# Two conditioned transformer layers in one kernel: set-up reordered and its weight handling moved into the steps

## The chip, the cores and the metric

The kernel runs on one core of a Trainium2 chip. The metric is the device time of one execution in microseconds. The core's engines are TensorE (PE: matrix products and transposes), VectorE (DVE), ScalarE (ACT), GpSimd (POOL) and SyncE (SP), which here only issues transfers (DMA). Each engine works through its own instructions in order and they meet through semaphores.

## What is computed

128 sequences of 64 tokens, 256 features, go through two layers. Both are attention with 16 heads of 16 features and a feed-forward part of width 1024, with a layer norm before each that is scaled and shifted by a condition vector (one of 256 features per sequence). All inputs are float32.

```python
# layer 0
gamma1 = cond @ g1_w + g1_b;  beta1 = cond @ b1_w + b1_b          # "modulation", also gamma2, beta2
alpha1 = tanh(cond @ a1_w + a1_b) * 0.1                           # "gate", also alpha2
y = layernorm(x, ln1_g, ln1_b) * (1 + gamma1) + beta1
x = x + attention(y, qkv_w, qkv_b, proj_w, proj_b) * alpha1
z = layernorm(x, ln2_g, ln2_b) * (1 + gamma2) + beta2
x = x + (gelu(z @ fc1_w + fc1_b) @ fc2_w + fc2_b) * alpha2
# layer 1
h = layernorm(x, ln1_g, ln1_b) * (1 + scale) + shift              # [shift, scale] = cond @ ada1_w + ada1_b
q, k = rotary(h @ wq + bq), rotary(h @ wk + bk);  v = h @ wv + bv
x = x + softmax(where(mask, q k^T / 4, -inf)) v @ wo + bo
x = x + gelu(ada_norm2(x) @ ff_w1 + ff_b1) @ ff_w2 + ff_b2
```

## The kernel before

**Precision.** Weights and activations are split in a high and a low part (`wgt_hi`, `wgt_lo`, `y_hi`, `y_lo` ...), and a product is three passes (helper `product`, L886). The high part of a weight is made by a copy on ScalarE (`high_weights`, L656 and L659), the low part by a subtraction on VectorE (`low_weights`, L1187 and L1191). `w_hi[n]` and `w_lo[n]` count what is done, with n = 0 for qkv, 1 for the projection, 2 for fc1 and 3 for fc2. A feed-forward matrix has 2048 columns per partition, the projection 512, qkv 1536. There is one copy of the split weights: layer 1's overwrite layer 0's.

**Tiling.** The 8192 tokens make 16 tiles of 512 (8 sequences) per layer, so 32 tiles in all, and `NT` = 16. Layer 0's result goes to memory (`mid`) and is read again by layer 1. A **step** u works on up to five tiles at once: it loads and normalises tile u+2 (argument `n`), makes y, queries, keys and values of tile u+1 (`a`), runs attention of tile u (`b`), feed-forward of tile u-1 (`c`) and finishes tile u-2 (`p`). Each argument is the layer of that tile, or None where there is no such tile. The order of all of it is written out by hand in one `step` function per engine. The whole kernel is, on every engine, `begin`, step -1, `second`, step 0, `third`, step 1, a loop over steps 2 to 13, steps 14 to 17, a loop over steps 18 to 29, and steps 30 to 33 (function `program`). Step -1 makes y, queries, keys and values of tile 0; step 0 is attention of tile 0 without any feed-forward; layer 1's tiles begin to appear as tile u+1 in step 15.

**Attention.** A tile has four groups of two sequences. Queries and keys of a group are spread into padded buffers by transfers: four for the keys (`spread_keys`, L418) and two for the queries (`spread_queries`, L426), with two sets of buffers, so groups 0 and 1 are sent at the end of the step before and groups 2 and 3 early in the step itself. The scores of a group (PE, `A<-k_pad,q_pad`) wait for them. Then come maximum (L1335) and subtraction (L1341) on VectorE, the exponential (L749) on ScalarE, transposes (L1022), a copy (L754), weighing of the values (L1036), normalising (L1359), a transpose of the heads (`turn_heads`, L1047), the projection, and the gated residual on VectorE.

**Set-up.** `begin` loads the condition, tile 0, weights, biases; makes the transposed condition, layer 0's first modulation (TensorE L897 into bank D0, VectorE `modulations`, L1199 to L1206) and the split of qkv. In `second` TensorE makes the gate products (L918, L919), the second modulation and a transpose of the mask (L924); ScalarE copies the projection, takes the tanh (L671) and copies fc1 and fc2 whole; VectorE subtracts the projection, makes the gates, the modulation and the mask, and subtracts fc1 and fc2 whole; SyncE writes the four gate rows and the mask to memory and waits for them (`rows_out`). The rows are broadcast back in every step of layer 0 (L444, L445, L476). In `third` layer 1's modulation weights and columns are loaded (L321 is the line of the small helper `ld` that most loads go through), its modulation is made, its qkv weights are sent for, and all engines wait for all of it before step 1.

**The turn to layer 1.** Layer 1's qkv is split in step 15 (`u == NT - 1`) before the first product of the feed-forward, the projection early in step 16. fc1 is split whole between two softmaxes of step 17, fc2 some 20 us later in that step.

## Time and profile before

| what | value |
|---|---|
| median of 3 runs | 1927.71 us (1926.1 to 1930.4) |
| profiled execution | 1930.19 us |
| its span | 1928.4 us, 41731 instructions |
| mean granted TensorE clock | 0.98 |
| PE busy | 1806.2 us (94%) |
| DVE, ACT, POOL busy | 1235.5 (64%), 1307.8 (68%), 849.7 us (44%) |
| chain that ended last | PE 66%, DVE 13%, issue 10%, POOL 7%, ACT 2% |
| queries to their buffer (`q_pad<-q_flat`) | 256 transfers of 128 KB, 2.3 us to landing |

Times in all views are in us from the start of the span. A row of a timeline gives the start, the duration, the engine, the line, the operation, what it writes and reads, how often (neighbours are merged), and in brackets how long the engine had been idle and who released it. Matrix products are pipelined, so a row's duration is a little longer than its share of the engine. The granted clock is a share of 2.4 GHz: 1.00 is that level all the time, 0.50 would be 1.2 GHz all the time.

### The profile page before, as it was taken

The page shows a single profiled execution, that of the slowest core. Times are in us where ns is not written, and L with a number is a line of the kernel's source. Part 1 is how long each engine was busy: PE and PEld are TensorE (multiplying, and loading weights), DVE is VectorE, ACT ScalarE, POOL GpSimd, SP SyncE. Part 2 cuts the span into 40 slices and gives each one's busy share as a digit, 9 for nine tenths or more (in the row PEclk, how much of TensorE's full clock was granted, in tenths as well). Part 3 has the DMA queues.
Part 4 walks back from the last instruction along what each step waited for, and adds up shares of the span by engine and source line. Part 5 has one row for each costly group of instructions (what it writes and reads, how often), then busy time and mean ns, then how long its engine had stood idle before and what let it go on. Part 6 is the DMA issues. An engine that isn't in the chain of part 4 may idle for free.

```text
span 1928.4 us, 41731 instructions
## 1 busy us (share of the span) xinstructions
PE 1806.2 (94%) x12623; PEld 1646.5 (85%) x12623; DVE 1235.5 (64%) x2973; ACT 1307.8 (68%) x2315; POOL 849.7 (44%) x1036
## 2 busy tenths in 40 slices
PE   5779999999999999999897999999999999999997
PEld 4668988888898888889787989999988998998985
DVE  5656666767666676766676567767666766766651
ACT  3347776776777677777666676776676677677663
POOL 2123333343333334334544565555555555556433
PEclk8879999999999999999998999999999999999999
DMA  6464434444443444543343233333323333332320
GB/s 162 110 138 103 102 97 114 120 121 129 104 100 98 111 120 122 128 107 96 109 142 95 73 93 103 97 102 106 92 81 104 97 96 105 110 82 85 98 60 33
DMA packets 330275, 199.84 MB, mean 104 GB/s; under 512 B 160994, under 2 KB 314596, under 8 KB 330212
## 3 DMA queue, kind: packets, MB, share of 16 engines
q1 hardware_dynamic: 330212, 199.06, 38.8%
q8 instruction: 32, 0.52, 0.1%
q14 instruction: 31, 0.25, 0.0%
HBM read 80.98 MB, written 17.33 MB: 51 GB/s over the span
## 4 chain that ended last, share of the span: by engine, by line
PE 66%; DVE 13%; issue 10%; POOL 7%; ACT 2%; DMA 1%; SPq 1%; DVEq 0%; POOLq 0%; ACTq 0%
PE D L886 16%; PE C L886 12%; PE A L886 12%; PE B L1036 7%; PE B L886 7%; PE B L1022 4%; PE E L886 3%; POOL h_lo L551 2%; DVE mx L1335 2%; POOL q_flat L597 2%; DVE o_sb L1359 2%; PE A L1008 2%; DVE exps L1341 1%; DVE ot_lo L1368 1%; PE E L1047 1%
## 5 line engine op out<-in xcount | busy, mean ns | idle before, releaser
L551 POOL TENSOR_TENSOR h_lo<-hact,h_hi 128x512 fp32r<-128x512 f32 x256 | 330.5, 1291 | 325.0 <-ACT h_hi L745 317.0
L886 PE MATMUL D<-wgt_hi,h_hi 128*128 128x256 f32 x1024 | 304.2, 297 | 27.3 <-POOL h_lo L551 18.6
L886 PE MATMUL D<-wgt_lo,h_hi 128*128 128x256 f32 x1024 | 290.7, 284 | 0.0
L886 PE MATMUL D<-wgt_hi,h_lo 128*128 128x256 f32 x1024 | 290.4, 284 | 0.0
L886 PE MATMUL A<-k_pad,q_pad 128*128 128x256 f32 x1536 | 260.9, 297 | 9.8 <-DVE mod L1206 4.7
L740 ACT ACTIVATE hact<-C,b_col 128x512 f32<-128x512 f32 x256 | 176.2, 688 | 124.0 <-PE C L886 121.8
L1036 PE MATMUL B<-v_blocks,probs_turned 128*128 128x68 f32 x2048 | 255.8, 272 | 0.0
L1036 PEld LDWEIGHTS B<-v_blocks,probs_turned 128*128 128x128 f32 x2048 | 250.7, 193 | 5.2 <-ACT probs_turned L754 2.5
L754 ACT COPY probs_turned<-B 128x512 f32<-128x512 f32 x256 | 147.8, 585 | 157.1 <-PE B L1022 157.0
L886 PEld LDWEIGHTS D<-wgt_hi,h_hi 128*128 128x128 f32 x1024 | 196.1, 191 | 44.5 <-POOL h_lo L551 29.8
L886 PEld LDWEIGHTS A<-k_pad,q_pad 128*128 128x128 f32 x1536 | 215.6, 195 | 13.8 <-DVE mod L1206 4.9
L1335 DVE TENSOR_REDUCE mx<-A 128x8 f32<-128x512 f32 x256 | 174.3, 681 | 79.2 <-PE A L1008 48.6
L886 PE MATMUL C<-z_hi,wgt_hi 128*128 128x512 f32 x512 | 210.6, 411 | 6.1 <-ACT hact L740 4.7
L749 ACT ACTIVATE exps<-exps 128x512 f32<-128x512 f32 x256 | 161.2, 630 | 79.7 <-DVE exps L1341 79.0
L886 PE MATMUL C<-z_hi,wgt_lo 128*128 128x512 f32 x512 | 201.1, 393 | 0.0
L886 PE MATMUL C<-z_lo,wgt_hi 128*128 128x512 f32 x512 | 200.5, 392 | 0.0
L886 PEld LDWEIGHTS D<-wgt_hi,h_lo 128*128 128x128 f32 x1024 | 196.7, 192 | 1.3
L886 PEld LDWEIGHTS D<-wgt_lo,h_hi 128*128 128x128 f32 x1024 | 196.3, 192 | 0.0
L1341 DVE TENSOR_TENSOR exps<-A,mx 128x512 f32<-128x512 f32 x256 | 173.9, 679 | 3.8 <-PE B L1022 0.5
L541 POOL TENSOR_SCALAR rs<-mv 128x1 f32<-128x1 f32 x128 | 30.0, 234 | 323.8 <-DVE mv L1392 321.2
L1022 PE MATMUL B<-ident,exps 128*128 128x128 f32 x1024 | 157.3, 277 | 8.4 <-DVE o_sb L1359 5.2
L1359 DVE TENSOR_TENSOR o_sb<-B,rden 64x128 f32<-64x128 f32 x512 | 146.5, 286 | 24.9 <-PE E L1047 7.7
(138 smaller groups left out, 4231.5 us busy)
## 6 DMA issues: line engine op xcount, KB each, us to landing
k_pad<-k_flat SPq DMA_DIRECT2D x512, 64.0 KB, 2.1
q_pad<-q_flat SPq DMA_DIRECT2D x256, 128.0 KB, 2.3
gates<-gates SPq DMA_DIRECT2D x64, 256.0 KB, 4.5
x_bias<-x_bias SPq DMA_DIRECT2D x32, 512.0 KB, 3.5
rotation<-rotation SPq DMA_DIRECT2D x256, 64.0 KB, 1.9
x_in<-in_x SPq DMA_DIRECT2D x16, 512.0 KB, 4.2
gates<-gated_bias SPq DMA_DIRECT2D x32, 256.0 KB, 4.9
x_res<-in_x SPq DMA_DIRECT2D x16, 512.0 KB, 4.2
```

Source lines behind the costliest of these rows:

```text
L551: pool.tensor_tensor(hb[1][:, m % 2, :], hact[:, m % 2, :], hb[0][:, m % 2, :].bitcast(F32), ALU.subtract).then_inc(h_lo, 1)
L597: pool.tensor_tensor(flat[keys][:, :, i % KC, 1, :], by_group(rot_sum[:, i % KC, :]), flat[keys][:, :, i % KC, 0, :].bitcast(F32), ALU.sub ...
L740: nc.scalar.activation(hact[:, m % 2, :], C[:, :], ACT.Gelu, bias=b1_col[:, layer, m:m + 1]).then_inc(gelu, 1)
L749: nc.scalar.activation(exps[:, b, :], exps[:, b, :], ACT.Exp, scale=SCORE_SCALE).then_inc(s_exp, 1)
L754: nc.scalar.copy(pt[:, b, :], B[b][:, :]).then_inc(pt_moved, 1)
L886: ins = nc.tensor.matmul(dst, l, r, start=first_start and n == 0, stop=last_stop and n == len(todo) - 1, **kw)
L1008: ins = nc.tensor.matmul(dst, mean_w[:, :], row, start=False, stop=True)
L1022: ins = nc.tensor.transpose(B[b][:, n * P:(n + 1) * P], exps[:, b, n * P:(n + 1) * P], ident[:, :])
L1036: ins = nc.tensor.matmul(B[b][:, n * 68:(n + 1) * 68], pt[:, b, n * P:(n + 1) * P], moving, start=True, stop=True)
L1335: nc.vector.tensor_reduce(mx[:, b, :], A[b][:, :].rearrange("p (h k) -> p h k", k=S), AX.X, ALU.max)\
L1341: nc.vector.tensor_tensor(exps[:, b, :].rearrange("p (h k) -> p h k", k=S), A[b][:, :].rearrange("p (h k) -> p h k", k=S), mx[:, b, :].rea ...
L1359: ins = nc.vector.tensor_tensor(o_sb[p, b, :].rearrange("p (n j d) -> p n j d", n=4, j=2), sums_of(b)[p, :, x, :, 0:HD], rden[p, b, :].rea ...
```

## The change

- **Loads of `begin`.** The mask is loaded early, qkv next, then the gate and second modulation weights ahead of the bias columns. Bias columns of the modulations get semaphores of their own (`cols_in`), which VectorE waits for and TensorE doesn't. fc1 and fc2 leave `begin` and are issued at the start of `second`, ahead of the gate rows.
- **GpSimd** clears the key buffers before the first layer-norm chain and not after it.
- **Step -1** takes over what `second` did: TensorE makes mask transpose, gate products and second modulation right after y's transposes and before the queries (`gate_products`); ScalarE casts qkv before it waits for the modulation; VectorE subtracts the query and key weights after y's shift, the value weights apart (`low_values`, semaphore `w_lo_v`), and makes mask and gates there (`gate_parts`). Group 0's queries are sent before group 1's keys. The mask goes to memory alone (`mask_out`).
- **Step 0** takes over what `third` did, and the feed-forward weights: layer 1's modulation weights and columns are loaded after group 3 (`modulation_weights`, 10 transfers, into other buffers), TensorE makes both modulations right after y's transposes, VectorE scales both modulations, and fc2 and fc1 are split in pieces of a quarter (512 columns, `high_piece`, `low_piece`) spread over the step. The load of `x1_bias` for tile 0 moves to its end.
- **Step 1** ends, on SyncE, with layer 1's 16 query and key columns (`layer_columns`); **step 14** ends with the other columns, rows and the qkv and projection weights (`layer_weights`), and ScalarE and VectorE split qkv at its end and not in the middle of step 15.
- **Steps 16 and 17** split layer 1's fc1 and fc2 in quarters: five at the end of step 16, three in step 17, each as soon as the last tile of layer 0 has used that quarter. TensorE waits per quarter.

```diff
@@ SyncE
             def begin():
                 ...
-                columns(mods_in[0], 0, 0, [w[0]["g1_b"], w[0]["b1_b"]])
+                columns(cols_in[0], 0, 0, [w[0]["g1_b"], w[0]["b1_b"]])
+                ld(mask_in, mask_u8[:, :], t["mask_BxS_bf1"])
                 ld(w_in[0], qkv, rows(w[0]["qkv_w"]))
-                qk_columns(0, [w[0]["qkv_b"][0:2 * D]])
-                other_columns(0, w[0]["qkv_b"][2 * D:3 * D], w[0]["fc1_b"])
-                projection(0, w[0]["proj_w"])
                 for n, m in enumerate(("a1", "a2")):
                     ld(gates_in, mod_raw[4 + n], rows(w[0][m + "_w"]))
                     ld(gates_in, gate_row[:, n, :], row(w[0][m + "_b"]))
+                for n, m in enumerate(("g2", "b2")):
+                    ld(mods_in[1], mod_raw[2 + n], rows(w[0][m + "_w"]))
+                qk_columns(0, [w[0]["qkv_b"][0:2 * D]])
+                projection(0, w[0]["proj_w"])
                 ld(gates_in, bias_rows[:, 0, :], w[0]["proj_b"].partition_broadcast(P))
                 ld(gates_in, bias_rows[:, 1, :], w[0]["fc2_b"].partition_broadcast(P))
                 ...
+                other_columns(0, w[0]["qkv_b"][2 * D:3 * D], w[0]["fc1_b"])
+                columns(cols_in[1], 0, 1, [w[0]["g2_b"], w[0]["b2_b"]])
+
+            def second():
+                ld(w_in[3], w_raw[2].rearrange("p (k n) -> p k n", k=MC), rows(w[0]["fc2_w"]))
                 ld(w_in[2], w_raw[1].rearrange("p (k n) -> p k n", k=KC), rows(w[0]["fc1_w"]))
                 ...
                 sp.wait_ge(gates_made, 4)
                 ...
-                sp.wait_ge(mask_made, 3)
-                ld(rows_out, mask_rows, mask_add)
-                sp.wait_ge(rows_out, 80)
-                sp.wait_ge(mod_done, 16)
+                sp.wait_ge(rows_out, 64)
+                sp.wait_ge(pe_mods, 2)
+
+            def modulation_weights():
+
+                sp.wait_ge(pe_gates, 1)
                 for n in range(2):
                     ld(mods_in[2], ada_raw[n], rows(w[1][f"ada{n + 1}_w"]))
                     ...
@@ SyncE, step
                     spread_keys(u, 3)
                     spread_queries(u, 3)
+                if known(u) and u == 0:
+                    modulation_weights()
                 ...
                     spread_keys(u + 1, 0)
-                    spread_keys(u + 1, 1)
+                    if not (known(u) and u == -1):
+                        spread_keys(u + 1, 1)
                     wait_apart(sp, sp_passed, (qk_hi, upto(u + 1, 4, 4)), low_done(u + 1, a, 4))
                     spread_queries(u + 1, 0)
+                    if known(u) and u == -1:
+                        spread_keys(u + 1, 1)
                     spread_queries(u + 1, 1)
+                if known(u) and u == 0:
+                    wait_apart(sp, sp_passed, (w_lo[3], 4))
+                    gated_bias(0)
+                if known(u) and u == 1:
+                    layer_columns()
+                if known(u) and u == NT - 2:
+                    layer_weights()
@@ ScalarE, step
-                if known(u) and u == NT - 1:
-                    act.wait_ge(pe_v, upto(NT, 2, 0))
-                    high_weights(0, 1)
                 ...
                 if c is not None:
                     hidden(u - 1, c, 2)
+                elif known(u) and u == 0:
+                    high_piece(3, 0, 0)
                 ...
+                if known(u) and u == NT - 2:
+                    act.wait_ge(pe_v, upto(NT, 2, 0))
+                    high_weights(0, 1)
+                if known(u) and u == NT:
+                    high_piece(3, 1, 1)
+                    high_piece(2, 1, 2)
                 if n is not None:
                     first_norm(u + 2)
                     first_columns(u + 2, n)
@@ TensorE, step
                 if a is not None:
                     first_turn(u + 1, 0, b)
                     first_turn(u + 1, 1, b)
+                if known(u) and u == -1:
+                    gate_products()
+                if known(u) and u == 0:
+                    pe.wait_ge(mods_in[2], 16 * 2)
+                    pe.wait_ge(mod_done, 16)
+                    for n in range(2):
+                        modulations(Dk[n], ada_raw[n][:, :, D:2 * D], ada_raw[n][:, :, 0:D])
                 if b is not None:
                     turn_heads(u, 1, c)
@@ VectorE
             def low_weights(n, layer):
                 dve.wait_ge(w_hi[n], layer + 1)
                 if n == 0:
-                    for kind in W_PIECES:
+
+                    for kind in W_PIECES[1 - layer:]:
                 ...
+            def low_piece(n, layer, q):
+                dve.wait_ge(w_hi[n], 4 * layer + q + 1)
+                nc.vector.tensor_tensor(ff_piece(n, wgt[1][:, W_AT[n]], q), ff_piece(n, w_source(n, layer), q),
+                                        ff_piece(n, wgt[0][:, W_AT[n]], q).bitcast(F32), ALU.subtract).then_inc(w_lo[n], 1)
@@ VectorE, step
+                if known(u) and u == NT:
+                    low_piece(2, 1, 0)
+                    low_piece(2, 1, 1)
+                    low_piece(3, 1, 0)
+                    low_piece(3, 1, 1)
+                    low_piece(2, 1, 2)
```

## Rows read from the trace of the kernel before

**Rows 1.** Stages: length; each engine's busy us; clock; DMA share; GB/s.

```profile
core 0: us, PE busy (x) PEld busy (x) DVE busy (x) ACT busy (x) POOL busy (x), PEclk, DMA share, GB/s
...
46.45:97.10 50.65, 37.92 (x232) 33.71 (x232) 34.64 (x80) 19.26 (x39) 7.28 (x14) 0.83 0.46 107
97.10:113.70 16.60, 6.75 (x33) 6.48 (x32) 5.83 (x20) 3.05 (x8) 3.36 (x4) 0.74 0.24 45
113.70:174.03 60.33, 57.63 (x367) 52.38 (x368) 35.36 (x88) 38.86 (x70) 15.88 (x23) 0.90 0.50 118
174.03:230.19 56.16, 54.44 (x386) 49.44 (x385) 37.53 (x92) 40.79 (x73) 20.80 (x27) 1.00 0.45 114
904.49:968.36 63.87, 57.49 (x389) 52.67 (x388) 43.06 (x101) 42.84 (x79) 32.12 (x40) 0.95 0.44 116
...
1028.08:1098.90 70.82, 59.88 (x403) 55.32 (x402) 43.34 (x94) 44.23 (x74) 33.55 (x39) 0.90 0.28 79
1098.90:1155.67 56.77, 55.68 (x403) 51.35 (x401) 37.77 (x90) 40.52 (x73) 31.70 (x39) 1.00 0.34 98
```

**Rows 2.** Timeline of TensorE in the set-up.

```profile
24.06 0.77 PE L886 MATMUL A<-y_hi,wgt_hi 128*128 128x512 f32 x1 [10.58 <-DVE y_lo L1282]
...
35.62 1.03 PE L918 MATMUL C<-gates,condT 128*128 128x256 f32 x4
...
38.89 2.05 PE L897 MATMUL D<-condT,gates 128*128 128x128 f32 x16
...
46.45 2.93 PE L886 MATMUL A<-k_pad,q_pad 128*128 128x256 f32 x12 [0.38 <-DVE maskT L1243]
```

**Rows 3.** Layer 0's modulation scaled on VectorE (line view), and GpSimd's memset (timeline).

```profile
L1206 DVE TENSOR_SCALAR mod<-mod,ln_col x4: 278/278/1905, 13.3 to 44.9; 128x128 f32<-128x128 f32 x4
...
13.19 1.92 POOL L516 MEMSET v_blocks<- 128x2176 f32 x1
```

**Rows 4.** Timeline of SyncE: the eight columns, and the first gate load.

```profile
5.28 5.22 SPq L321 DMA_DIRECT2D qk_bias<-in_L_cond_qkv_b  x8
...
47.02 0.66 SPq L444 DMA_DIRECT2D gates<-gates  x1
```

**Rows 5.** DMA issues up to 125 us: count, KB each, us to landing.

```profile
q_pad<-q_flat SPq DMA_DIRECT2D x14, 128.0 KB, 2.4
...
x_bias<-in_L_cond_fc_w SPq DMA_DIRECT2D x1, 1024.0 KB, 9.3
...
rotation<-in_L_cond_ada_w SPq DMA_DIRECT2D x2, 512.0 KB, 3.7
...
mask_u<-in_mask_BxS_bf SPq DMA_DIRECT2D x1, 8.0 KB, 9.0
```

**Rows 6.** Timeline of TensorE in step 0 and before step 1.

```profile
59.24 0.96 PE L886 MATMUL A<-k_pad,q_pad 128*128 128x256 f32 x6
...
102.36 6.67 PE L897 MATMUL D<-condT,rotation 128*128 128x128 f32 x32 [5.17 <-DMA mod_col<-in_L_cond_ada_b]
113.70 1.65 PE L886 MATMUL A<-k_pad,q_pad 128*128 128x256 f32 x6 [4.67 <-DVE mod L1206]
```

**Rows 7.** Timelines about a step's end: SyncE, ScalarE, VectorE.

```profile
890.78 2.78 SPq L426 DMA_DIRECT2D q_pad<-q_flat  x4
902.12 0.65 SPq L444 DMA_DIRECT2D gates<-gates  x1
...
851.17 0.63 ACT L749 ACTIVATE exps<-exps 128x512 f32<-128x512 f32 x1
...
917.98 1.86 ACT L656 CAST wgt_hi<-w_raw 128x512 fp32r<-128x512 f32 x5
...
1155.87 0.69 DVE L1335 TENSOR_REDUCE mx<-A 128x8 f32<-128x512 f32 x1 [3.16 <-PE A L1008]
```

**Rows 8.** Timelines of step 17: ScalarE and VectorE.

```profile
1034.33 1.90 ACT L659 CAST wgt_hi<-w_raw 128x2048 fp32r<-128x2048 f32 x1
...
1036.27 2.29 DVE L1191 TENSOR_TENSOR wgt_lo<-w_raw,wgt_hi 128x2048 fp32r<-128x2048 f32 x1 [2.95 <-ACT wgt_hi L659]
...
1058.62 2.26 DVE L1191 TENSOR_TENSOR wgt_lo<-gates,wgt_hi 128x2048 fp32r<-128x2048 f32 x1
```

212 lines of the change are left out of this document (133 added, 79 removed).

## Prediction

> **What bounds the kernel now.** I read the stages first [rows 1]. From 174 us on a tile of layer 0 takes 56.16 us, in 54.44 of which TensorE is busy at full clock, and one of layer 1 takes 56.77: there TensorE is the bound, and the change adds and removes next to no product. What it can win lies where TensorE waits. That is four places: the set-up up to the first scores at 46.45 us; step 0 (50.65 us long, 37.92 busy, clock 0.83); 16.60 us between its last product and step 1, with 6.75 busy; and steps 15 and 17 at the turn to layer 1 (63.87 and 70.82 us, 7.1 and 14.1 over the steady 56.77). I then read TensorE's own idle rows in the set-up [rows 2], who disturbs VectorE there [rows 3], SyncE's queue [rows 4, 7] and the landings [rows 5], since all transfers go through that one queue.
>
> **Set-up, before the first scores.** TensorE idles 10.58 us until y is made at 24.06 [rows 2]. Three edits shorten y's path. TensorE's modulation product no longer waits for the bias columns (0.7 us, from the 4 column loads issued after the two weights). One VectorE instruction of layer 0's modulation took 1.91 us where its three twins take 0.28, over the very time of a 1.92 us memset on GpSimd [rows 3]; with the key memsets moved to the start, that overlap goes: 1.6 us. The subtraction of the query and key weights (1.4 us) comes after y's scale and shift, not before, so it moves but stays on the path; only the values' part leaves it. Together y is ready near 19.8. But the gate products now stand ahead of the queries in TensorE's order, and their semaphore counts six transfers, the two broadcast bias rows among them. In SyncE's new order these come behind the 8 query/key columns, which alone cost 5.22 us of issue [rows 4]; adding up the queue, they are issued by 15.6 and land near 18.9. The products took 3.3 us at full clock (35.62 to 38.89); at 1.2 GHz, where TensorE starts after such a wait, 1.6 times that (32 products in 6.67 us against 16 in 2.05) [rows 2, 6]: 5.4, and the second modulation 2.05. So queries begin at about 26.5, 2.4 us later than now; they then run at full clock and end with the values near 35.5, where they end now. Up to here nothing is won. What is won is the stretch from 35.62 to 46.45 [rows 2]: products, mask and the two whole-matrix subtractions are gone from it, and the group's queries are sent ahead of the second group's keys. First scores: about 37.5, 9 us earlier.
>
> **The same 9 us, lost again.** fc2 and fc1 (1 MB each) are now issued near 39.7, directly ahead of the four gate rows; SyncE waits for those rows before it issues anything of step 0. In the trace an 8 KB mask issued behind the same two weights took 9.0 us to land, as long as the weight ahead of it (9.3) [rows 5]. So the rows land near 50.3; now SyncE goes on at 47.02 [rows 4]. Then come, at 0.66 us of issue each, four gate loads, the third group's four keys and two queries, 6.6 us, and the last lands 2.4 later [rows 5]: 59.4 with the small gaps between. The third group's scores run at 59.24 now [rows 6]. TensorE gets there 9 us early and stands still. Gain at this point: 0 (below: 0 if rows drain faster is wrong; above: 7, if the small rows overtake the weights). I take 0 by the mask row. The Trainium skill (DMA: Bandwidth & Descriptors, Queues, rings and completion order) says that each DMA engine consumes its ring's descriptors in order while completion is not first-in first-out for the issuing engine; by the first half the 9 us are lost, by the second some could stay, and the mask row speaks for the first.
>
> **Step 0, second half.** TensorE now stops after y's transposes until layer 1's two modulation weights are in. SyncE issues them behind the fourth group (near 62.0), the second one five issues later, landing 3.7 us on [rows 5]: 68.9, where TensorE arrives at 67 to 68. The products take 3.4 us at full clock, 6.67 at 1.2 GHz [rows 6]. Everything queued behind them waits: the second group's heads, and through them VectorE, whose shifts for y stand behind those heads. Shift against now: 5 to 8 us, I take 5.1. On VectorE come layer 1's 16 modulation instructions (4.67 us, as long as TensorE waits for them now) [rows 6] and layer 0's eight, half that: the eight fall into the wait for the third group and cost nothing; the 16 are half hidden while TensorE makes the first keys, and eight pieces of 512 columns at about 0.65 us (a quarter of the 2.29 us whole [rows 8], plus start-up), half hidden in its idle time; on ScalarE eight pieces of about 0.55, mostly hidden. That is 3.5 more: step 0 ends 8.6 us later than now, near 105.7.
>
> **Between step 0 and 1.** The 16.60 us go entirely: 5.17 waiting for a column, 6.67 of products, 4.67 waiting for VectorE [rows 6]. Step 1 starts at 105.7 instead of 113.7, gain 8.0. It loses 0.8 again, since normalising tile 2 and two pieces now stand right ahead of its first softmax, and wins 4: step 1 runs at clock 0.90 now [rows 1], 10% of 60 us in slow columns, and would start at full clock. **Gain of set-up, step 0 and step 1 together: 11** (3 to 22; the lower end if TensorE runs the modulation slowly and each piece shows in full, the upper if the rows overtake).
>
> **Columns in step 1.** Sixteen issues are twice the 5.22 us row, 10.4 us, where SyncE idles from 893.56 to 902.12 in a steady step, 8.6 us [rows 4, 7]. The overhang of 1.9 delays gate loads and the third group's keys; the latter wait for scores anyway. Cost 0.3 (0 to 2).
>
> **Steps 14 and 15.** Layer 1's query, key and value cast leaves the middle of step 15, where VectorE is full; I put half of the 7.1 us excess on it, 3.9 (3 to 4.5). It now stands at the end of step 14 on ScalarE, ahead of the normalisation, the gelu and the first exponential, and ScalarE has no gap there: the exponential at 851.17 follows its table load at once [rows 7]. Cast 1.86 us [rows 7], plus some 0.8 waiting: SyncE issues six columns and rows and then the three weights after 893.6, to land near 903. Cost 2.7. Net gain 1.2 (-1 to 4).
>
> **Steps 16 and 17.** Step 16 keeps its own excess (the projection's weights are cast in it as before). In step 17 the whole-matrix cast (1.90) and subtraction (2.29) of fc1 sit between two softmaxes, and fc2's subtraction (2.26) holds the first product back [rows 8]. In pieces, five are done at the end of step 16, where VectorE idles 3.16 us before the next tile's maximum [rows 7]: five at 0.65 are 3.3, cost 0.1, and 0.6 for ScalarE's two. Of the three left, two casts (1.1) fall before an exponential that is not waited for yet, and the subtractions follow y, where VectorE idles for the keys. Left of the 14.1: 1.1. Gain 13 (10 to 14).
>
> **Sum.** 11 - 0.3 + 1.2 + 13 = 25 us. The profiled execution takes 1930.19 (span 1928.4 and 1.8 around it), so 1905; the median of the three runs is 2.5 below it: 1903.
>
> **Rivals.** (1) *The rows overtake, or the two weights drain in half the time*: third group at 52.4 instead of 59.4, the modulation weights 7 earlier, all before it hidden: gain 32, 1896. For: the weights arrive from memory while rows leave for it; against: the mask row. (2) *The turn to layer 1 is not bound by the casts*: the piecewise work at the ends of steps 14 and 16 pushes ScalarE's gelus into the next softmax, and clock drops follow as after 24.06; gain there 4, and 11 - 0.3: 15, 1913. For: ScalarE without a gap [rows 7]; against: VectorE's 3.16 us, and that the two long stalls sit right at the whole-matrix rows. (3) *Slower than before*: TensorE stopped in order for the modulation weights. Price: each us that they land after 68.9 is one us on step 0, with 14 won at the turn and 11 here it decides from 25 us on, i.e. landing after 94. For: ten issues behind three queues' worth of spreads; against: 3.7 us landing. (4) *Pieces do not replace the stall but share it*, gain 3 to 10, 1922. A rule of the Trainium skill (SBUF — State Buffer, SBUF: two separate sides) says that VectorE and GpSimd take a shared port pair by an exclusive lock and the loser blocks. The 1.91 us row agrees. By it the reordered memsets win only what [rows 3] shows, so it changes no rival.
>
> **How the numbers follow.** Forecast (gain 18 to 32) 0.60; rival 1 and beyond 0.14; rival 2 0.14; rival 4 0.05; within 0.2% (3.9 us, about what a measurement of this kernel can tell) 0.04; rival 3 or another cause of a slower kernel 0.03. Range: from the upper end of rival 1 with the turn in full (gain 40, 1888) to a little past rival 2 (gain 11, 1917). Faster 0.93, same 0.04, slower 0.03.
>
> **What would show it.** First scores near 37.5; TensorE idle some 9 us before the third group's scores, which stay near 59; a wait of TensorE on the second modulation weight of 1 to 3 us; step 1 from about 106 at clock near 1; step 15 near 62.5, step 16 as long as before, step 17 near 58 us. Wrong it would be if step 0 lengthens beyond 75 us from the first scores, or if a steady step changes from 56.16 or 56.77 at all, since thirty of them outweigh everything here.

## Result and profile after

| | before | after |
|---|---|---|
| median of the timed runs | 1927.62 us (8 runs, 1924.98 to 1931.4) | 1921.01 us (8 runs, 1919.7 to 1922.54) |
| profiled execution, span | 1930.19, 1928.4 us | 1919.92, 1918.1 us |
| granted clock | 0.980 | 0.986 |

The ratio is 0.9964, 95% interval 0.9955 to 0.9973: the change makes the kernel 6.6 us faster. The forecast was 1903 us with a range from 1888 to 1917. The direction was right, the size was not: 25 us were expected. One execution of one experiment (layer 1's modulation weights in front) was slow, 2479 us at a granted clock of 0.65, and stands in no median.

Stages of the kernel after. The columns are those of [rows 1]; the stretches are the set-up up to the first scores, step 0 up to the third group's scores, the rest of step 0, step 1, a steady step of layer 0, then steps 15, 17, 18, a steady step of layer 1, and step 31.

```profile
core 0: us, PE busy (x) PEld busy (x) DVE busy (x) ACT busy (x) POOL busy (x), PEclk, DMA share, GB/s
0.00:41.12 41.12, 25.05 (x103) 19.87 (x104) 20.53 (x53) 13.37 (x27) 9.29 (x18) 0.83 0.45 115
41.12:62.92 21.80, 6.67 (x52) 6.09 (x52) 8.96 (x22) 6.26 (x12) 0.73 (x3) 0.80 0.82 218
62.92:112.78 49.86, 35.69 (x212) 31.84 (x213) 31.35 (x86) 19.33 (x40) 7.30 (x14) 0.85 0.34 83
112.78:170.63 57.85, 54.25 (x369) 48.59 (x367) 37.77 (x94) 41.84 (x79) 19.80 (x27) 0.97 0.40 101
170.63:226.83 56.20, 54.49 (x387) 49.42 (x385) 37.56 (x92) 40.79 (x73) 20.77 (x27) 1.00 0.46 116
901.17:966.61 65.44, 57.63 (x388) 52.41 (x387) 43.89 (x101) 45.16 (x85) 32.66 (x40) 0.95 0.44 115
1026.35:1084.03 57.68, 55.83 (x402) 51.38 (x401) 40.57 (x96) 42.23 (x76) 33.55 (x41) 1.00 0.36 96
1084.03:1143.18 59.15, 57.05 (x403) 52.84 (x402) 37.79 (x90) 40.40 (x73) 31.01 (x39) 0.97 0.33 95
1199.94:1256.70 56.76, 55.71 (x403) 51.37 (x402) 37.76 (x90) 40.42 (x73) 31.72 (x39) 1.00 0.34 97
1823.62:1875.43 51.81, 48.43 (x339) 43.64 (x338) 27.26 (x68) 31.71 (x52) 18.19 (x21) 0.97 0.19 52
```

The steady steps are what they were (56.20 against 56.16 us, 56.76 against 56.77), so the difference lies in the stages around them. A step is counted from its first transposes of `zn` on TensorE to the next step's, and step 1 from its first scores (113.70 before, 112.78 after):

| stage | forecast gain | gain in the two traces |
|---|---|---|
| up to step 1 | 8.0 | 0.9 |
| step 1 | 3.2 (and -0.3 for the columns) | 2.5 |
| steps 2 to 14 | 0 | 0 |
| steps 14/15 | 1.2 | -1.6 |
| step 17 | 13 | 13.1 |
| step 18 | 0 | -2.4 |
| steps 19 to 30 | 0 | -0.7 |
| step 31 | 0 | -1.6 |
| sum | 25 | 10.2 |

Two things blur this balance. The set-up's length varies from one execution to the next: in the four profiles with the set-up of the kernel after (one of them with 48 empty instructions in it) the first scores of step 1 come between 111.1 and 116.4 us, and in the kernel before and one that shares its set-up at 113.7 and 110.3. So the 0.9 us of the table lie within this spread. And in step 31 the granted clock falls to 0.92 and 0.73 in two 5 us slices without any new wait, which happened in the profiles of some kernels and not in others with the same code there. The profiled execution of the kernel before is 2.6 us above its median, that of the kernel after 1.1 below its own. The medians, 6.6 us apart, say more than the 10.3 of the two profiled executions.

**The set-up of the kernel after.** Timeline of TensorE (start, duration, operation; in brackets the idle time before it and what ended it), then the issues of SyncE, and of the view of the DMA issues up to 125 us the landings of the gate rows.

```profile
20.14 2.05 PE L983 MATMUL C<-gates,condT 128*128 128x256 f32 x4 [7.04 <-DMA exps<-in_L_cond_fc_b]
...
26.42 3.78 PE L959 MATMUL D<-condT,gates 128*128 128x128 f32 x16
29.85 0.62 PE L948 MATMUL A<-y_hi,wgt_hi 128*128 128x512 f32 x1
...
41.12 1.66 PE L948 MATMUL A<-k_pad,q_pad 128*128 128x256 f32 x12 [2.09 <-issue]
...
62.92 1.65 PE L948 MATMUL A<-k_pad,q_pad 128*128 128x256 f32 x6 [10.32 <-DMA q_pad<-q_flat]
```

```profile
43.41 0.64 SPq L329 DMA_DIRECT2D x_bias<-in_L_cond_fc_w  x1
44.10 0.64 SPq L329 DMA_DIRECT2D rotation<-in_L_cond_fc_w  x1
44.79 0.47 SPq L329 DMA_DIRECT2D gates<-hact  x1
...
53.57 0.65 SPq L464 DMA_DIRECT2D gates<-gates  x1
```

```profile
gates<-hact SPq DMA_DIRECT2D x2, 128.0 KB, 7.3
```

TensorE waits 7.04 us for the bias rows before the gate products, runs these and the second modulation at 1.2 GHz (16 products in 3.78 us; the same took 2.05 in [rows 2]), and starts the queries at 29.85. The gate rows then stand behind the 2 MB of fc2 and fc1, take 7.3 us to land, and SyncE does not go on before 53.57 (47.02 in [rows 4]). So the third group's scores come at 62.92, 3.7 us later than before [rows 6].

**The rest of step 0.** TensorE's waits, and the one of VectorE behind the last of them:

```profile
73.23 2.05 PE L959 MATMUL D<-condT,rotation 128*128 128x128 f32 x16 [0.95 <-DMA gates<-in_L_cond_ada_w]
...
82.75 0.77 PE L948 MATMUL A<-y_hi,wgt_hi 128*128 128x512 f32 x1 [3.06 <-DVE y_lo L1350]
...
104.63 0.39 PE L948 MATMUL B<-wgt_hi,y_hi 128*128 128x256 f32 x1 [3.20 <-DVE o_sb L1427]
```

```profile
102.59 0.69 DVE L1267 TENSOR_TENSOR wgt_lo<-rotation,wgt_hi 128x512 fp32r<-128x512 f32 x1 [1.30 <-ACT wgt_hi L688]
```

VectorE works in order: y's low part stands behind the heads and layer 1's modulation (3.06 us of TensorE), and the normalised heads stand behind a piece that ScalarE has not cast yet (3.20 us).

**The boundary of steps 14 and 15.** Timelines of ScalarE, VectorE, GpSimd and TensorE, two slices of 5 us, and the line view of the subtraction (ns, min/median/max of its five instructions):

```profile
901.15 1.87 ACT L694 CAST wgt_hi<-w_raw 128x512 fp32r<-128x512 f32 x5 [2.43 <-DMA w_raw<-in_L_cond_wv]
...
903.06 3.70 DVE L1254 TENSOR_TENSOR wgt_lo<-w_raw,wgt_hi 128x512 fp32r<-128x512 f32 x5 [3.44 <-ACT wgt_hi L694]
...
902.47 2.40 POOL L592 TENSOR_TENSOR x_bias<-x_bias,x_res 128x1024 f32<-128x1024 f32 x1
...
908.70 1.62 PE L948 MATMUL A<-k_pad,q_pad 128*128 128x256 f32 x6 [4.43 <-DVE exps L1409]
...
915.37 0.61 PE L1014 MATMUL E<-ident,zn 128*128 128x128 f32 x4
...
905.45:910.45 5.00, 1.75 (x8) 1.78 (x9) 4.99 (x11) 4.04 (x7) 1.29 (x1) 0.69 0.80 199
910.45:915.45 5.00, 5.00 (x31) 5.00 (x30) 3.83 (x8) 2.78 (x5) 2.37 (x1) 0.62 0.13 30
...
L1254 DVE TENSOR_TENSOR wgt_lo<-w_raw,wgt_hi x5: 411/414/2353, 903.1 to 906.3; 128x256 fp32r<-128x256 f32 x4, 128x512 fp32r<-128x512 f32 x1
```

Four of the five subtractions take 0.41 us, one takes 2.35, over the time of GpSimd's sum of x_bias and x_res. TensorE waits 4.43 us for subtracted scores (the granted clock is 0.69 and 0.62 in the two 5 us slices from 905.45 on, some 3.4 us more), and its second set of transposes of this step (915.37) starts 14.2 us after the step's start; in the kernel before it was 7.3 us. In the traces that have the same code here, the five subtractions take between 2.93 and 5.28 us, as they meet GpSimd's instructions, and step 15 between 64.8 and 67.1 us: its 65.4 is one value of a spread. The stall in the middle of step 15, in the kernel before and in the kernel after:

```profile
927.78 0.55 PE L886 MATMUL E<-wgt_hi,ot_hi 128*128 128x256 f32 x1 [3.38 <-DVE ot_lo L1368]
```

```profile
928.35 0.35 PE L948 MATMUL E<-wgt_hi,ot_hi 128*128 128x256 f32 x1 [0.36 <-DVE ot_lo L1436]
```

### The profile page after: what moved, and what is told of

It is laid out like the page before. It is cut to its first block, busy times and chain, and to the rows that moved or that the text cites. A ratio compares the mean times of both kernels' runs of the same rounds, so it can differ in the third digit from the quotient of the medians.

```text
span 1918.1 us, 41774 instructions
## 1 busy us (share of the span) xinstructions
PE 1801.9 (94%) x12623; PEld 1641.1 (86%) x12623; DVE 1236.7 (64%) x2985; ACT 1307.9 (68%) x2327; POOL 848.8 (44%) x1036
## 4 chain that ended last, share of the span: by engine, by line
PE 65%; DVE 11%; issue 9%; POOL 6%; SPq 4%; DMA 3%; ACT 2%; DVEq 0%; POOLq 0%; ACTq 0%
PE D L948 16%; PE C L948 12%; PE A L948 11%; PE B L1093 7%; PE B L948 7%; PE B L1079 4%; PE E L948 3%; POOL h_lo L581 2%; DVE mx L1403 2%; POOL q_flat L627 2%; DMA rotation<-rotation 2%; DVE o_sb L1427 2%; PE A L1065 2%; DVE exps L1409 1%; SPq L449 1%
## 5 line engine op out<-in xcount | busy, mean ns | idle before, releaser
L948 PEld LDWEIGHTS A<-k_pad,q_pad 128*128 128x128 f32 x1536 | 212.5, 192 | 26.7 <-DMA q_pad<-q_flat 14.2
L776 ACT CAST h_hi<-hact 128x512 fp32r<-128x512 f32 x256 | 159.4, 623 | 4.2
```

The source lines that it names most:

```text
L776: nc.scalar.copy(hb[0][:, m % 2, :], hact[:, m % 2, :]).then_inc(h_hi, 1)
L948: ins = nc.tensor.matmul(dst, l, r, start=first_start and n == 0, stop=last_stop and n == len(todo) - 1, **kw)
```

## Experiments

All are edits of the kernel after unless said otherwise. The ratio is to the kernel before in the same series, with its 95% interval. The interval of a median of four is some 3 us to either side (6.5 for both repairs of SyncE's order together), so two experiments are told apart only where they differ by more; where the text gives a smaller difference, it says so or goes by the traces.

### The turn to layer 1 alone

The kernel before, with layer 1's fc1 and fc2 weights handled in quarters in steps 16 and 17 as in the kernel after, and nothing else of the change:

```diff
                 if known(u) and u == NT + 1:
-                    act.wait_ge(pe_f1, upto(NT, MC, 0))
-                    high_weights(2, 1)
+                    high_piece(2, 1, 3)
+                    high_piece(3, 1, 2)
...
+                if known(u) and u == NT:
+                    high_piece(2, 1, 0)
+                    high_piece(2, 1, 1)
```

> The kernel before, with one part of the change alone: layer 1's fc1 and fc2 are split in quarters at the end of step 16 and in step 17. Theory 1 (the turn to layer 1 wins its 13 us, and set-up and step 15 together give back most of that): step 17 falls from 70.8 to 57.5-58 us, all other steps keep their length, median near 1914.5, faster than the whole change (1921.0). Theory 2 (the traces overstate the turn, since their difference, 10.3 us, is larger than that of the medians, 6.6): median near 1918-1921.

Measured: 1918.06 us (1917.07 to 1919.85), ratio 0.9954 (0.9937 to 0.997). Steps 17 and 18:

```profile
1027.23:1084.83 57.60, 55.84 (x403) 51.39 (x402) 40.55 (x96) 42.34 (x76) 33.51 (x41) 1.00 0.34 97
1084.83:1144.25 59.42, 57.03 (x403) 52.84 (x402) 37.82 (x90) 40.41 (x73) 31.05 (x39) 0.97 0.32 94
```

Step 17 wins 13.2 us as in theory 1, step 18, which theory 1 left alone, loses 2.7, and the median is that of theory 2: 9.3 us are won. The whole change gives 6.6. The intervals of the two ratios overlap, so it is not shown that everything else in the change is a loss (3 us by the medians), but nothing of the 12 us expected from it is seen in the medians.

### fc1's and fc2's weights in front again

```diff
             def begin():
...
                 columns(cols_in[1], 0, 1, [w[0]["g2_b"], w[0]["b2_b"]])
+                ld(w_in[3], w_raw[2].rearrange("p (k n) -> p k n", k=MC), rows(w[0]["fc2_w"]))
+                ld(w_in[2], w_raw[1].rearrange("p (k n) -> p k n", k=KC), rows(w[0]["fc1_w"]))
             def second():
-                ld(w_in[3], w_raw[2].rearrange("p (k n) -> p k n", k=MC), rows(w[0]["fc2_w"]))
-                ld(w_in[2], w_raw[1].rearrange("p (k n) -> p k n", k=KC), rows(w[0]["fc1_w"]))
                 sp.wait_ge(gates_made, 4)
```

> The changed kernel, with the loads of fc2 and fc1 back at the end of the first block of loads, as in the kernel before, so that nothing large stands ahead of the gate rows. Theory 1 (the rows wait behind the two weights in the queue): gate rows land 1.8 us after issue and not 7.3, the third group's scores start near 57 and not 62.9, and step 1 some 5-6 us earlier; median near 1915. Theory 2 (TensorE's in-order stop for the modulation weights takes over): third group near 57, but step 1 only 0-2 us earlier, median 1919-1921.

Measured: 1914.36 us (1912.74 to 1916.64), ratio 0.9938 (0.9922 to 0.9955): 6.6 us less than the kernel after, theory 1.

```profile
55.95 1.65 PE L948 MATMUL A<-k_pad,q_pad 128*128 128x256 f32 x6 [3.71 <-DMA q_pad<-q_flat]
```

The third group's scores come 7.0 us earlier (62.92 before this edit), and TensorE's wait for them goes from 10.32 to 3.71 us. The gate rows land in 2.0 us instead of 7.3 and step 1 starts 7.3 us earlier: they did stand behind the 2 MB.

### The bias rows ahead of what does not need to be early

```diff
+                ld(gates_in, bias_rows[:, 0, :], w[0]["proj_b"].partition_broadcast(P))
+                ld(gates_in, bias_rows[:, 1, :], w[0]["fc2_b"].partition_broadcast(P))
                 for n, m in enumerate(("g2", "b2")):
                     ld(mods_in[1], mod_raw[2 + n], rows(w[0][m + "_w"]))
                 qk_columns(0, [w[0]["qkv_b"][0:2 * D]])
                 projection(0, w[0]["proj_w"])
-                ld(gates_in, bias_rows[:, 0, :], w[0]["proj_b"].partition_broadcast(P))
-                ld(gates_in, bias_rows[:, 1, :], w[0]["fc2_b"].partition_broadcast(P))
```

> The changed kernel, with the two broadcast bias rows loaded ahead of the second modulation's weights and of the eight query/key columns. Theory 1 (queries are late because the gate products stand ahead of them and wait for these rows): gate products start near 14 and not 20.1, still at 1.2 GHz, queries near 24 and not 29.85, and everything up to step 1 comes 5-6 us earlier; median near 1915.5. Theory 2 (the columns, now later by about 1 us, or the DMA queue hold the first scores): queries earlier but first scores and step 1 unchanged, median 1920-1921.

Measured: 1913.09 us (1910.01 to 1914.63), ratio 0.993 (0.9914 to 0.9947): 7.9 us less than the kernel after.

```profile
14.32 1.10 PE L983 MATMUL C<-gates,condT 128*128 128x256 f32 x4 [0.98 <-DMA exps<-in_L_cond_fc_b]
...
17.66 2.05 PE L959 MATMUL D<-condT,gates 128*128 128x128 f32 x16
...
32.05 1.66 PE L948 MATMUL A<-k_pad,q_pad 128*128 128x256 f32 x12 [3.44 <-issue]
...
52.42 1.65 PE L948 MATMUL A<-k_pad,q_pad 128*128 128x256 f32 x6 [9.53 <-DMA q_pad<-q_flat]
```

The wait for the bias rows goes from 7.04 to 0.98 us, TensorE is then at full clock for the gate products and the modulation (the expectation had 1.2 GHz), and the first scores come 9.1 us earlier. The third group still waits 9.53 us: this edit moves the stage, it does not remove the transfers' stop.

### Both repairs of SyncE's order

> The kernel after, with both repairs of SyncE's order together: fc1's and fc2's weights issued at the end of the first set-up stage, and the two bias rows that the gate products wait for issued ahead of the modulation weights and the eight columns. Theory 1, the two losses lie one behind the other (gate products and queries start 6 us late, and then the gate rows stand behind 2 MB in the queue), so the gains add: 6.6 and 7.9 us, a median near 1906.5, step 1 starting near 100 us. Theory 2, both repairs shorten the same wait (that of the third group's scores for the gate rows' transfers), so together they give hardly more than the larger: 1911 to 1913, step 1 at 104 to 106 us.

Measured: 1904.44 us (1903.78 to 1914.61), ratio 0.9897 (0.9863 to 0.9931): 16.6 us less than the kernel after, as much as the two apart (6.6 and 7.9) and a little more; three executions lie within 1.3 us, the fourth 10 above. Step 1 starts at 98.9 us (first scores). The gains add: two waits one behind the other.

### Layer 1's weights loaded in the middle of step 14

```diff
                 if b == 0 and not (known(u) and u == 0):
                     gated_bias(u)
+                if known(u) and u == NT - 2:
+                    layer_weights()
...
                 if known(u) and u == 1:
                     layer_columns()
-                if known(u) and u == NT - 2:
-                    layer_weights()
```

> The changed kernel, with layer 1's other columns and its qkv and projection weights sent for in the middle of step 14, in SyncE's idle stretch, and not at its end. Theory 1 (a good part of the stall at the start of step 15 is ScalarE waiting for the weights, 2.4 us): ScalarE's idle time before the cast goes, step 15 falls from 65.4 to 62-63 us, median near 1918. Theory 2 (the cast and the 3.7 us subtraction alone make the stall, the wait is covered): step 15 stays above 64.5, median 1920-1921.

Measured: 1919.18 us (1917.81 to 1919.46), ratio 0.9957 (0.994 to 0.9973), 1.8 us less than the kernel after, which the intervals do not tell from nothing. ScalarE's wait of 2.43 us for the weights is gone, but VectorE's five subtractions now take 5.31 us together, and step 15 is 64.2 us instead of 65.4, between the two theories. Then the same on top of both repairs of SyncE's order:

> The kernel before this one in the same call, and layer 1's columns and weights issued in SyncE's idle stretch in the middle of step 14. Theory 1, ScalarE's wait of 2.4 us for the value weights goes and TensorE starts step 15 some 2 us earlier: 1.8 to 2.5 us under the run with both repairs alone. Theory 2, VectorE's subtraction is held by GpSimd's two-operand instruction over the same stretch (one piece of it took 2.35 us in the kernel after and 2.60 us with the early load, where the others take 0.41) and eats what the earlier landing gives: within 1 us of the run with both repairs alone, with one piece of the subtraction at 1.3 us or more.

Measured: 1900.26 us (1899.11 to 1900.82), ratio 0.986 (0.9841 to 0.9879), 4.2 us less than without the load (the intervals overlap). The line view of the subtraction there:

```profile
L1254 DVE TENSOR_TENSOR wgt_lo<-w_raw,wgt_hi x5: 417/691/2602, 886.5 to 889.2; 128x256 fp32r<-128x256 f32 x4, 128x512 fp32r<-128x512 f32 x1
```

Both theories are half right. Step 15 is 62.2 us instead of 64.8 (theory 1), and one piece takes 2.60 us (theory 2). But some 1.6 us of that step are the clock's: it stays at 1.00 here, while three other traces with the same early load and the same subtraction (5.30 or 5.31 us) have a fall at the same wait or right behind it and take 63.8 to 64.2 us. Of the 5.3 us between this trace and the one without the load, 2.6 are step 15's; 1.3 are step 18's (57.93 instead of 59.19) and 1.5 step 31's clock.

### GpSimd quiet while VectorE subtracts

The kernel with both repairs and the early load (1900.3 us), with GpSimd's order changed at the start of step 15:

```diff
-                if c is not None:
+                if c is not None and not (known(u) and u == NT - 1):
                     x1_bias(u - 1, c)
+                if known(u) and u == NT - 1:
+                    pool.wait_ge(w_lo[0], 2)
                 if p is not None:
                     hidden_low(u - 2, MC - 1)
+                if known(u) and u == NT - 1:
+                    x1_bias(u - 1, c)
```

> The kernel with both repairs of SyncE's order and layer 1's weights loaded in the middle of step 14 (1900.3 us median, step 15 62.2 us), and at the start of step 15 GpSimd waits for VectorE's subtraction of layer 1's query, key and value weights, then does its last subtraction of tile 13 and only after it the sum of x_bias and x_res (2.57 us) that stood in front. Theory 1, the VectorE subtractions are held while GpSimd runs an instruction with two operands from SBUF: with GpSimd quiet the five pieces take 2.0 to 3.0 us where they took 5.31, none of them over 1.5, the first scores of step 15 start 2 to 3 us earlier and the median is 1897 to 1898.5. Theory 2, the long piece has a cause of its own on VectorE (its operands, or ScalarE's normalization beside it): the five pieces take 4.5 us or more again, and the median is 1900 to 1901.5, since GpSimd's order gives nothing and delays its last subtraction by some 0.5 us.

Measured: 1899.27 us (1897.13 to 1901.81), ratio 0.9852 (0.9835 to 0.9868). GpSimd's and VectorE's rows at the boundary, and the line view:

```profile
887.37 1.46 POOL L581 TENSOR_TENSOR h_lo<-hact,h_hi 128x512 fp32r<-128x512 f32 x1
...
891.13 2.36 POOL L592 TENSOR_TENSOR x_bias<-x_bias,x_res 128x1024 f32<-128x1024 f32 x1
...
886.33 3.12 DVE L1258 TENSOR_TENSOR wgt_lo<-w_raw,wgt_hi 128x512 fp32r<-128x512 f32 x5 [0.90 <-ACT wgt_hi L698]
...
L1258 DVE TENSOR_TENSOR wgt_lo<-w_raw,wgt_hi x5: 415/420/1504, 886.3 to 889.0; 128x256 fp32r<-128x256 f32 x4, 128x512 fp32r<-128x512 f32 x1
```

The hold of theory 1 is shown: the five take 3.12 us instead of 5.31, and the longest is now 1.50, over GpSimd's remaining instruction of 1.46. Step 15 goes from 62.2 to 60.1 us, both at a granted clock of 1.00, and TensorE's longest wait at its start goes from 3.00 to 0.81. The median is above the 1898.5 of theory 1: only 1.0 of the gain can be seen, inside the spread of both, since step 18 went back from 57.9 to 59.0 (next but one experiment).

### The split back in the middle of step 15

ScalarE's part; VectorE's `low_weights(0, 1)` moves in the same way.

```diff
-                if known(u) and u == NT - 2:
-                    act.wait_ge(pe_v, upto(NT, 2, 0))
-                    high_weights(0, 1)
...
+                if known(u) and u == NT - 1:
+                    act.wait_ge(pe_v, upto(NT, 2, 0))
+                    high_weights(0, 1)
                 if known(u) and u == NT + 1:
                     high_piece(3, 1, 3)
```

> The kernel after, with layer 1's query, key and value weights split in the middle of step 15 again (the casts on ScalarE and the subtractions on VectorE where the kernel before had them), everything else as in the kernel after. Theory 1, the move of the split to the end of step 14 is a loss: its weights land after step 14's last products, so TensorE stops some 6 us between steps 14 and 15, and what it gives back in the middle of step 15 is some 4.5 us. Undone, step 15 goes from 65.4 back to 63.9 us and the median from 1921.0 to about 1919.4. Theory 2, the move is worth what the prediction gave it or more (the boundary costs 2.7, the middle gives back 3.9): undone, step 15 is 66.6 us or longer and the median is 1922 to 1924.

Measured: 1919.11 us (1917.68 to 1919.8), ratio 0.9956 (0.9942 to 0.9971), 1.9 us less than the kernel after.

```profile
904.30:968.12 63.82, 57.45 (x389) 52.29 (x387) 42.98 (x101) 42.91 (x79) 32.86 (x40) 0.95 0.45 118
```

Step 15 is 63.8 us, as in the kernel before: against the 65.4 of the kernel after, the move is a loss of 1.6 us in the traces, and against the five traces with the same code there one of 1.0 to 3.3. The medians do not tell the two kernels apart. With the early load and a quiet GpSimd the same move is a gain (60.1 us against 63.8).

### TensorE's code blocks shifted

```diff
                 pe.wait_ge(cond_turned, 1)
+                for _ in range(48):
+                    pe.sem_inc(pe_blank, 1)
                 pe.wait_ge(mods_in[0], 16 * 2)
```

> The kernel after, with 48 empty instructions (increments of a semaphore that nobody reads) put into TensorE's program in the set-up, ahead of its wait for the first modulation weights. Nothing in step 18 changes but where in its program TensorE's code blocks begin. In the first step of layer 1's loop (step 18) the profile has three packets of 16 KB in the instruction queue, at 10, 28 and 43.5 us from the step's start in the kernel after and at 12, 28 and 44.1 us in the kernel before; the last rotary swap of the step, issued until 42.9, lands by 44.4 us in the kernel before and at 46.0 in the kernel after. Theory 1, the code packet stands ahead of the swap's last packets on one of the DMA engines, and this is what makes step 18 last 59.2 us where it lasted 56.8: shifted by 48 instructions (3 us) the packet misses the swap, GpSimd's wait for it goes from 1.8 to 0.2 us and step 18 is 56.7 to 57.0 us. Theory 2, the loss comes from the piecewise turn of layer 1's weights in steps 16 and 17: step 18 stays at 59.0 to 59.4 us.

Measured: 1913.89 us (1912.08 to 1918.44), ratio 0.9928 (0.9909 to 0.9947). In step 18 the third packet of the instruction queue comes at 41.7 us from the step's start instead of 43.5. GpSimd's row that waits for the last swap and TensorE's that waits for GpSimd, in the kernel after and here, and steps 2 and 18 here:

```profile
1130.07 1.26 POOL L621 TENSOR_TENSOR rotation<-rotation 128x512 f32<-128x512 f32 x1 [1.79 <-DMA rotation<-rotation]
...
1132.60 0.57 PE L948 MATMUL D<-wgt_hi,h_hi 128*128 128x256 f32 x1 [1.86 <-POOL h_lo L581]
```

```profile
1131.29 1.28 POOL L621 TENSOR_TENSOR rotation<-rotation 128x512 f32<-128x512 f32 x1 [0.91 <-DMA rotation<-rotation]
...
1133.84 0.39 PE L948 MATMUL D<-wgt_hi,h_hi 128*128 128x256 f32 x1 [1.00 <-POOL h_lo L581]
...
180.53 1.46 PE L948 MATMUL A<-k_pad,q_pad 128*128 128x256 f32 x6 [2.44 <-DMA q_pad<-q_flat]
...
168.60:227.74 59.14, 55.88 (x387) 50.99 (x386) 37.77 (x92) 40.80 (x73) 20.72 (x27) 0.97 0.43 111
1086.14:1143.59 57.45, 55.77 (x402) 51.38 (x401) 37.78 (x90) 40.52 (x73) 31.70 (x40) 1.00 0.34 97
```

Step 18 is 57.45 us instead of 59.15, though nothing in it was changed. The wait halves rather than vanishes, so the expected 57.0 was a little too good. And not all of the 1.7 us is the packet's: the granted clock is 0.97 in step 18 of the kernel after and 1.00 here, and two kernels without the shift (both repairs with the early load, and all three edits together) have no fall there either and take 57.9 and 58.3 us, with waits of TensorE of 1.48 and 1.80. In the twelve traces with a changed turn and no shift this wait lies between 1.48 and 2.28 us, here it is 1.00, before the change 0.47. What was not expected speaks for the packet more plainly: step 2, the first pass of layer 0's loop, is now 59.14 us instead of 56.20. Its first packet comes at 8.9 us from its start instead of 12.4, and right there TensorE waits 2.44 us for padded queries where it waited 0.77. Three packets in a first pass, none in the passes after it. The median is 7.1 us below the kernel after's, clear of the intervals; the two traces are only 1.5 us apart, since the profile fell on the slowest of the four executions (1918.44, the others 1912.1 to 1914.5). Where the 7 us lie is open.

### The second modulation behind the queries, and layer 1's modulation weights in front

Both on the kernel with the two repairs and the early load (1900.3 us).

```diff
                 ins.then_inc(pe_gates, 1)
-                pe.wait_ge(mods_in[1], 16 * 2)
-                modulations(Dk[1], mod_raw[2], mod_raw[3])
             def second():
+                pe.wait_ge(mods_in[1], 16 * 2)
+                modulations(Dk[1], mod_raw[2], mod_raw[3])
                 pe.wait_ge(mask_turned, 1)
```

> The kernel with both repairs of SyncE's order and layer 1's weights loaded in the middle of step 14 (1900.3 us median), with TensorE's 16 products of layer 0's second modulation (18.40, 3.78 us at a granted clock of 1.2 GHz there, 2.05 us in the run without the early load) put behind the query, key and value products of step -1 instead of in front of them. Theory 1, TensorE is the last thing that the queries wait for (y's low part is ready at 18.8, the queries start at 21.8), and behind the value products TensorE waits 2.7 us for the padded keys and queries anyway: queries at 18.8 to 19.5, first scores 2 to 3 us earlier, a median of 1897 to 1899. Theory 2, the products only change places: SyncE's transfers of keys and queries start when VectorE is done with them and the stage is bound by these transfers and by the gate rows, whose issue waits for these products, so the first scores gain but the third group's scores do not, and the median stays within 1 us of 1900.3.

Measured: 1904.43 us (1902.47 to 1906.78), ratio 0.988 (0.9864 to 0.9897). TensorE starts the queries at 19.14, 2.7 us earlier, and the first scores come at 34.13 instead of 33.77, so the earlier queries win nothing, as theory 2 has it in the main. What follows the queries is SyncE's issue of keys and queries and their landing. Theory 2 had the median within 1 us of the base, and it is 4.2 above (the intervals overlap). The traces are 2.7 apart: step 15 is 63.8 us instead of 62.2 and step 18 59.0 instead of 57.9. In step 15 it is the clock; the base first, then this kernel:

```profile
893.75 0.94 PE L948 MATMUL A<-k_pad,q_pad 128*128 128x256 f32 x6 [3.00 <-DVE exps L1409]
896.42:901.42 5.00, 5.00 (x47) 4.98 (x44) 4.74 (x13) 2.27 (x5) 2.36 (x1) 1.00 0.26 59
...
893.77 0.95 PE L948 MATMUL A<-k_pad,q_pad 128*128 128x256 f32 x6 [2.99 <-DVE exps L1409]
896.45:901.45 5.00, 5.00 (x34) 5.00 (x34) 3.71 (x10) 1.73 (x4) 2.35 (x1) 0.72 0.25 56
```

After the same wait TensorE, busy all the time in both, keeps 2.4 GHz in one and has 1.2 GHz for a part of the slice in the other. What decides between the two is not shown.

```diff
                 if known(u) and u == -1:
                     wait_apart(sp, sp_passed, (mask_made, 3))
                     ld(mask_out, mask_rows, mask_add)
+                    modulation_weights()
...
-                if known(u) and u == 0:
-                    modulation_weights()
```

> The kernel with both repairs of SyncE's order and layer 1's weights loaded in the middle of step 14 (1900.3 us median), with layer 1's modulation weights and columns (1 MB and eight column loads, some 5 us of SyncE) issued in step -1, right behind the mask row, instead of in step 0. Theory 1, this queue position costs: the ten issues and the megabyte stand in front of the first keys and queries, whose copies are ready from 26.7 us on, so the first scores come 3 to 6 us later, and what is gained (TensorE's wait of 0.5 us for these weights in step 0, and 5 us of SyncE there) is less: 1902 to 1905. Theory 2, SyncE is idle from 23.2 to 26.7 us and takes most of it there, and in step 0 the loads of the next tile come 5 us earlier: 1897 to 1900.

Measured: 1911.65 us (1909.23 to 1912.36), ratio 0.9909 (0.989 to 0.9929). First scores at 39.58 (33.77), step 1 at 105.9 (99.3). The first scores come 5.8 us later, as theory 1 has it, but the median is worse than either theory had it. The ten issues end at 33.3 us; the keys have been ready since 26.7. The two traces are 11.9 us apart: 6.6 lie before step 1, the other 5 in steps 15, 18 and 31, which the edit does not touch and where the granted clock falls here and not in the base.

All three together (quiet GpSimd, late modulation, early modulation weights):

> The three edits of this call together on the kernel with both repairs and the early load. If each of the first two gives its 2 to 3 us, since they lie in different stages, and the early modulation weights cost 2 to 4: 1897 to 1900. If none does anything: 1900 to 1901. If all three help: 1893 to 1895.

Measured: 1905.07 us (1903.31 to 1905.97), ratio 0.9877 (0.986 to 0.9893), 4.8 us above the base: none of the three cases expected it. Step 15 keeps its gain (60.4 us) and the set-up keeps its loss (step 1 at 106.4).

## Why the prediction was wrong, point by point

**The steps that failed, in short.** Of the 15 us missing in the trace, 7.1 lie before step 1: terms of the set-up and of step 0 that were costed too small. 4.2 lie at the boundary of steps 14 and 15, where VectorE's subtraction was costed at nothing and ScalarE's wait at a third of what it was (5.3 won behind it where 3.9 were expected takes 1.4 of that back). 4.7 lie in steps 18 to 31, which the prediction took as unchanged.

**The queries' start: right mechanism, wrong sizes.** Forecast 26.5, measured 29.85. The bias rows landed 1.2 us later than the sum over the queue gave (20.14 against 18.9). The gate products took 6.3 us, not 5.4. And the 16 products of the second modulation took 3.4 us at 1.2 GHz (26.42 to 29.85), where the working used the 2.05 us of full clock although it had just put the same engine at 1.2 GHz. That is an error within the prediction: a stretch that was costed at the slow clock was followed by one at the fast clock for no stated reason. With it the first scores come at 41.12, forecast 37.5.

**The gate rows behind 2 MB: right.** Forecast: SyncE goes on 10.6 us after fc2's issue (39.7 to 50.3). Measured: 43.41 to 53.57, 10.2 us. TensorE was said to stand still 9 us before the third group's scores, and stood 10.32. The rival in which the rows overtake the weights is refuted by this, and the run with the weights in front shows the price: 6.6 us. The rule that a ring's descriptors are consumed in order, which the prediction took from the Trainium skill (DMA: Bandwidth & Descriptors, Queues, rings and completion order), agrees with the 7.3 us landing and with 2.0 us once the weights stood in front.

**The second half of step 0: too small a term.** From the third group's scores to step 1 it was to take 46.3 us (59.4 to 105.7), and took 49.9. The modulation weights cost 0.95 us of waiting as forecast (1 to 3), and TensorE made the products at full clock there. The term that failed is "mostly hidden" for ScalarE's pieces: one that waited behind a copy of probabilities held VectorE for 1.30 us and TensorE for 3.20. Together with the late third group (62.92 against 59.4) this makes step 1 start at 112.8, 7.1 us after the forecast; the gain of 8.0 became 0.9, and with the spread of the set-up it may be nothing.

**Step 1: nearly right.** 2.5 us gained of the 2.9 that are left after the columns, at clock 0.97.

**Steps 14 and 15: wrong in sign.** The stall in the middle of step 15 did go (TensorE's wait of 3.38 us for the heads in the kernel before is 0.36), and 5.3 us were won behind the boundary where 3.9 were expected. (The 3.9 was called half of an excess of 7.1, which is 3.6.) But the boundary costs 6.9 us, not 2.7. The prediction costed ScalarE's cast (1.86, measured 1.87) and its wait for the weights (0.8, measured 2.43) and did not cost VectorE's subtraction at all, which stands in front of the first maximum; it is 3.70 us long, where five pieces of 0.41 would make some 2, because GpSimd runs x_bias at that time. Nor did it cost the low clock behind the stall.

**Step 17: right.** 13.1 of 13.

**Step 18: not seen.** 2.4 us are lost in a step that the change does not touch. TensorE waits 1.86 us for GpSimd's h_lo there, where it waited 0.47, and the granted clock falls behind it. The run with the shifted code blocks makes the packets of TensorE's code the likely cause of the longer wait; why the change lengthened it and what decides the fall of the clock stay open. The trace of before held the three packets, and nobody would have read a cost out of them.

**The rivals.** Rival 4 gives the nearest number (gain 3 to 10, 1922), for a reason that step 17 refutes: the pieces did replace the stall. Rival 2 (1913) is refuted where it says that the turn was not bound by the casts; the clock drops that it feared did come, but behind the boundary of steps 14 and 15. Rival 3 is refuted by the wait of 0.95 us. The 15 us missing in the trace are 7.1 before step 1, 0.4 in it, 2.8 at steps 14 and 15 and 4.7 in steps 18 to 31.

**The better version.** Three moves in SyncE's program and one wait on GpSimd turn the change's 6.6 us into 29: 1899.27 us against 1928.16 for the kernel before in the same series, or 1900.26 without GpSimd's edit, with a narrower spread.

## What to carry to other kernels

When work is moved to an earlier place, write down the issuing queue's new order and ask of every transfer what large one stands in front of it and what waits for it: both repairs here are a few loads put in another place, and they are worth more than the whole change. Cost a moved step on every engine that takes part in it, the second one too, with the neighbours that will run beside it at the new place. And carry a clock assumption through to the next wait, not to the next line. Where two traces differ in a step that the edit does not touch, look at the granted clock there before you look for a cause.

## What was not expected of the hardware

**VectorE's subtraction is held for GpSimd's whole instruction.** With both operands in SBUF, one piece takes 1.50, 2.35 and 2.60 us, where its neighbours take 0.4 to 0.7, beside GpSimd instructions of 1.46, 2.40 and 2.57 us; moving the GpSimd instruction away ends it. The kernel before had it too: in the middle of its step 15 one of the same five pieces takes 1.50 us beside a GpSimd instruction of 1.48. A short one (0.60 us, `nb<-mv,rs`) beside a piece of 0.42 shows no hold. The Trainium skill (SBUF — State Buffer, SBUF: two separate sides) describes an exclusive lock on a shared port pair that lasts for the whole instruction; these rows agree, and the prediction, which had cited it, did not use it for the moved subtraction.

**Loading code can delay a transfer that TensorE waits for.** In the first pass of each loop the instruction queue carries three packets of some 16 KB; 48 empty instructions ahead brought one of them 1.8 us and one 3.5 us nearer to their step's start, step 18 became 1.7 us shorter (a part of it the clock's) and step 2 2.9 us longer. The Trainium skill (Runtime: NRT & Kernel Launch, Instruction fetch mechanics) says that code comes in blocks of 16 KiB and that crossing into one is mostly hidden. For TensorE's own stream that may hold; here it is the padded queries and the rotary swaps that came late. That the packet and the transfer meet on one DMA engine is argued from the times alone.
